# The chosen expert's weights reach the working buffers by SP transfers within SBUF instead of by VectorE copies

## The chip, the cores and the metric

One core of one Trainium2 chip runs the whole kernel. The metric is the device time of one execution in microseconds (us), the median of the runs shown. Engines are named as in the profile: PE (TensorE matmul), PEld (its weight load), DVE (VectorE), ACT (ScalarE), POOL (GpSimd), SP (SyncE, which here only issues transfers).

## The reference, cut to what matters

The input is x[16, 256, 128], 4096 tokens of 128 numbers, in fp32. A first layer (a diagonal linear recurrence over the sequence, a hidden layer of 512 with tanh-gelu, a residual, a layer norm) makes x1. A second layer is a mixture of experts:

```python
logits = xf @ Wg                       # 4096 x 8
probs = softmax(logits)
weights, indices = top_k(probs, 2)
for e in range(8):
    h = gelu(xf @ W1[e] + b1[e])       # 128 -> 512, exact gelu
    y = h @ W2[e] + b2[e]              # 512 -> 128
    out = out + y * cw[:, e:e + 1]     # cw: the two chosen weights of a token, else 0
return _layernorm(x + out)
```

## The kernel before, in words

**First layer.** Eight chunks of 512 tokens pass through `chunk(c)` on every engine. Beside them POOL splits the weights of all eight experts into a high and a low fp32r part (`weights(n)`, L410) and leaves them in one SBUF tensor, `fw[128, 8, 4*512]`: for each expert W1 high, W1 low, W2 high, W2 low. Every matmul of the kernel with these weights is three matmuls (`products`, L1015 to L1018): high by high, high by low, low by high.

**Routing.** It is done in two parts, the first 3 chunks (12 blocks of 128 tokens) and the last 5 (20 blocks). DVE finds the two chosen experts of each token and gives each (token, choice) a slot in a list sorted by expert (`route_choice`, `route_hits`, `route_ranks`, `route_slots`, `route_weights`, `route_experts`, L757 to L844). An expert's list is cut into tiles of SLOTS = 384 rows; the first part has 15 tiles, the second 21, so MT = 36, and each tile belongs to one expert. `route_experts` writes `experts`, one integer for each tile that packs the experts of tiles g, g+1 and g+2 in base 8.

**Dispatch.** POOL sends each block's rows to their slots in `slots_d` in HBM by indirect DMAs, two for each block (`dispatch`, L428 to L432): 24 in part 0, mixed with norms and weight splits, then 40 in part 1, all in a row (L460 to L463), once `routed` stands at 2 (L834) and all rows are there.

**Expert tiles.** Tile g uses the buffers of parity k = g % 2. SP loads its rows into `xb[:, k]` (`load`, L327 to L331). PE transposes them (`xt`), ACT and DVE split them into high and low (`x_high` L505, `x_low` L899), PE makes four hidden blocks (`hidden`, L1105) with `wuse[k]` planes 0 and 1, ACT applies the bias and the gelu (L569) and a high part (L574, every other one L911 on DVE), DVE the low part (L915), PE the product with W2 (L1133) with planes 2 and 3. ACT adds the output bias (L556), PE transposes back (L1119), ACT scales the rows by their routing weight into a ring `yo` of 21 tiles (L585), and POOL sends them back to `results_d` by three indirect DMAs a tile (`send_back`, L434 to L438), in order of tiles, after all 64 dispatches.

**Order.** Each engine's order is written by hand in a `step(g, ...)` of its own, walked by `walk` (L1169): steps 0 to 3 and the last ones unrolled, the others in loops of two. Routing of the second part is cut in before steps 1, 2, 3 and 4 (DVE: L957, ACT: L604). PE works one tile ahead: in step g, between the second and third W2 product of tile g, come the first two hidden blocks of tile g+1.

**The weights of a tile.** The two working buffers `wuse[0]` and `wuse[1]` (128 x 4 x 512 fp32r, 1 MB each) hold the weights of the even and the odd tile. In DVE's step g, after its work on hidden block 1, `weights2(g+1)` (L885) copies the two W2 planes of tile g+1 and the five bias columns into `buse`; after block 3, `weights1(g+2)` (L881) copies the W1 planes of tile g+2. Each `part_of_weights` (L876 to L879) is one DVE copy of 128 x 1024 fp32r; there are 72. The expert's number comes from `dve.value_load` of `experts` (L870). PE waits for `w1use_ready` before the first hidden block of a tile and for `w2use_ready` before its first W2 product. `wuse[1]` holds the first layer's weights until its last chunk is done.

**End.** SP waits until all send-backs have landed (`returned`, L355 to L361) and loads the two result rows of each token; PE, DVE, POOL and ACT add them, take the last layer norm, and SP stores. Of the results, chunks 0 to 2 need tiles 0 to 14 only and are fetched early; chunks 3 to 7 wait for the last send-back (L359).

Of the kernel before, what the change touches and what calls it, by code (L numbers as in the profile page):

```python
# [24 lines left out]
P = 128  # L25
F32 = mybir.dt.float32
# [11 lines left out]
E = 8  # L38
# [25 lines left out]
def build(nc, x, nu_log, theta_log, B_re, B_im, C_re, C_im, D_mat, W1, W2, res_logit,  # L64
# [20 lines left out]
    with ctx:  # L85
# [106 lines left out]
        expert = sb("expert", [P, MT + 2])  # L192
        pair = sb("pair", [P, MT])
        experts = sb("experts", [P, MT], I32)

        ht_h = [h_h[:, b, 0:SLOTS] for b in range(HB)]
        ht_l = [h_l[:, b, 0:SLOTS] for b in range(HB)]
# [10 lines left out]
        def y01(c):  # L208
# [18 lines left out]
            rt_ready row0_ready row1_ready lg_ready lg_sb  # L227
            hits_ready rank_ready rank_sb xin_ready xex_ready routed route_ready
            dispatched0 dispatched1 prefilled bias_loaded biasT_ready fbias_ready
            xTb_ready meta_ready w1use_ready w2use_ready xb_hi xb_lo preb_ready gelu_b hbh_ready hbh1_ready hbl_ready  # L230
            zb_ready yt_ready yT_ready yo_ready
            f_sum f_r f_st f_mv f_ve f_rstd f_nmr f_res f_res_last""".split()
        sm = {n: sem(n) for n in names}
        xr_loaded = [sem(f"xr_loaded{i}") for i in range(2)]
        fst_loaded = [sem(f"fst_loaded{i}") for i in range(2)]
        xb_loaded = [sem(f"xb_loaded{i}") for i in range(2)]

        kept = MT - YO
        GROUP = kept // 3
# [33 lines left out]
        def _(sp):  # L273
# [56 lines left out]
                wait(sp, sm["meta_ready"], g - 1)  # L330
                sp.dma_start(xb[:, k], slots_d[bass.ds(g * SLOTS, SLOTS), :].rearrange("(q p) r -> p q r", p=P)).then_inc(xb_loaded[k], 16)  # L331

            def loads(a, b):
                if (b - a) % 2:
                    load(a, a % 2)
                    a += 1
                with sp.Fori(0, (b - a) // 2) as i:
                    for k in range(2):
                        load(2 * i + (a + k), (a + k) % 2)


            sp.wait_ge(sm["dispatched0"], 16 * 2 * tiles[0])
            load(0, 0)
            load(1, 1)
            loads(2, slot0[1])
            sp.wait_ge(sm["dispatched1"], 16 * 2 * tiles[1])
            loads(slot0[1], MT)

            def results(c):

# [131 lines left out]
        def _(act):  # L482
# [76 lines left out]
            def step(g, k, now, prev, nxt, far, nth):  # L559


                if prev and not now:
                    evacuate(g - 1, 1 - k)
                if now:
                    act.wait_ge(sm["w2use_ready"], g + 1)
                    for b in range(HB):
                        act.wait_ge(sm["preb_ready"], HB * g + (b + 1))
                        wait(act, sm["hbl_ready"], HB * g + (b - 1))
                        act.activation(h32[:, b % 2, 0:SLOTS], H_PS[b % 2][:, 0:SLOTS], ACT.Gelu,  # L569
                                       bias=buse[:, k, b:b + 1]).then_inc(sm["gelu_b"], 1)  # L570
                        if b % 2 == 0:
                            act.wait_ge(sm["gelu_b"], HB * g + (b + 1))
                            wait(act, sm["zb_ready"], HB * g + (b + 1 - HB))
                            act.copy(ht_h[b], h32[:, b % 2, 0:SLOTS]).then_inc(sm["hbh_ready"], 1)  # L574
                        if b == 1 and prev:
                            evacuate(g - 1, 1 - k)
                        if b == 1 and nxt:
# [41 lines left out]
        def _(dve):  # L619
# [216 lines left out]
            def route_experts(p):  # L836

                M, g0 = slots[p], slot0[p]
                link(dve.tensor_tensor(cmp[:, 0:M, :], jio[:, 0:M].rearrange("p (m a) -> p m a", a=1).to_broadcast([P, M, E]),
                                       cnt[:, 3:4, :].to_broadcast([P, M, E]), ALU.is_ge))  # L840
                link(dve.tensor_reduce(ej[:, 0:M], cmp[:, 0:M, :], AX_X, ALU.add))
                link(dve.tensor_scalar(expert[:, g0:g0 + M], ej[:, 0:M], float(E - 1), None, ALU.min))
                link(dve.scalar_tensor_tensor(out=pair[:], in0=expert[:, 1:MT + 1], scalar=float(E), in1=expert[:, 2:MT + 2], op0=ALU.mult, op1=ALU.add))
                dve.scalar_tensor_tensor(out=experts[:], in0=expert[:, 0:MT], scalar=float(E * E), in1=pair[:], op0=ALU.mult, op1=ALU.add).then_inc(sm["route_ready"], 1)  # L844

# [27 lines left out]
                e = dve.value_load(at, min_val=0, max_val=E * E * E - 1)  # L873
                return [e // (E * E), (e // E) % E, e % E]

            def part_of_weights(k, e, a):  # L876

                return dve.tensor_copy(wuse[k][:, 2 * a:2 * a + 2, :].rearrange("p a h -> p (a h)"),  # L878
                                       fw[:, bass.ds(e, 1), 2 * a * H:2 * (a + 1) * H].rearrange("p a h -> p (a h)"))  # L879

            def weights1(g, k, e):  # L881
                wait(dve, sm["preb_ready"], HB * (g - 1))
                part_of_weights(k, e, 0).then_inc(sm["w1use_ready"], 1)

            def weights2(g, k, e):  # L885
                wait(dve, sm["zb_ready"], HB * (g - 1))
                part_of_weights(k, e, 1)
                wait(dve, sm["yt_ready"], g - 1)
                dve.tensor_copy(buse[:, k, :], fbias[:, bass.ds(e, 1), :].rearrange("p a b -> p (a b)")).then_inc(sm["w2use_ready"], 1)

            def meta(g, k):

# [12 lines left out]
            def step(g, k, now, prev, nxt, far, nth):  # L905
                if now:
                    for b in range(HB):
                        if b % 2:
                            dve.wait_ge(sm["gelu_b"], HB * g + (b + 1))
                            wait(dve, sm["zb_ready"], HB * g + (b + 1 - HB))  # L910
                            dve.tensor_copy(ht_h[b], h32[:, b % 2, 0:SLOTS]).then_inc(sm["hbh1_ready"], 1)  # L911
                            dve.wait_ge(sm["hbh1_ready"], 2 * g + (b // 2 + 1))
                        else:
                            dve.wait_ge(sm["hbh_ready"], 2 * g + (b // 2 + 1))
                        dve.tensor_tensor(ht_l[b], h32[:, b % 2, 0:SLOTS], ht_h[b].bitcast(F32), ALU.subtract).then_inc(sm["hbl_ready"], 1)  # L915
                        if b == 0 and nxt and nth != 1:

                            held[:] = experts_of(g + 1)
                        e = held[1:] if nth == 1 else held
                        if b == 1 and nxt:  # L920
                            x_low(g + 1, 1 - k)
                            weights2(g + 1, 1 - k, e[0])
                            meta(g + 1, 1 - k)
                        if b == 3 and far:
                            weights1(g + 2, k, e[1])

            for c in range(NCH):
                chunk(c)
                if c == NCH - 2:
                    dve.wait_ge(sm["fw_lo"], NFW)  # L930
                    dve.wait_ge(sm["route_ready"], 1)
                    e = experts_of(0)
                    weights1(0, 0, e[0])
                    weights2(0, 0, e[0])

            logits(NCH - 1)
            route_choice(1, 0)
            x_low(0, 0)
            weights1(1, 1, e[1])
            meta(0, 0)  # L940
            route_choice(1, 1)

# [54 lines left out]
        def _(pe):  # L997
# [100 lines left out]
            def xt(g, k):  # L1098
# [3 lines left out]
                    last = pe.transpose(XTB_PS[:, q * P:(q + 1) * P], xb[:, k, q, 0:D], ident[:])  # L1102
                last.then_inc(sm["xTb_ready"], 1)

            def hidden(g, k, b):  # L1105

                wait(pe, sm["gelu_b"], HB * g + (b - 1))
                products(H_PS[b % 2][:, 0:SLOTS], wuse[k][:, 0, b * P:(b + 1) * P], wuse[k][:, 1, b * P:(b + 1) * P],
                         xbt_h[k], xbt_l[k], True, True).then_inc(sm["preb_ready"], 1)

            def step(g, k, now, prev, nxt, far, nth):
# [7 lines left out]
                        last = pe.transpose(YB_PS[1 - k][:, q * D:(q + 1) * D], yt[:, q * P:(q + 1) * P], ident[:])  # L1119
                    last.then_inc(sm["yT_ready"], 1)  # L1120
                if now:
                    pe.wait_ge(sm["w2use_ready"], g + 1)
                    for b in range(HB):
                        if b == 2 and nxt:

                            pe.wait_ge(sm["w1use_ready"], g + 2)
                            pe.wait_ge(sm["xb_lo"], g + 2)
                            hidden(g + 1, 1 - k, 0)
                            hidden(g + 1, 1 - k, 1)
                        if b == 3 and far:  # L1130
                            xt(g + 2, k)
                        pe.wait_ge(sm["hbl_ready"], HB * g + (b + 1))
                        products(ZB_PS[k][:, 0:SLOTS], wuse[k][:, 2, b * D:(b + 1) * D], wuse[k][:, 3, b * D:(b + 1) * D],  # L1133
                                 ht_h[b], ht_l[b], b == 0, b == HB - 1).then_inc(sm["zb_ready"], 1)
# [3 lines left out]
                chunk(c)  # L1138
            logits(NCH - 1)
            xt(0, 0)  # L1140
            pe.wait_ge(sm["w1use_ready"], 1)
            pe.wait_ge(sm["xb_lo"], 1)
            hidden(0, 0, 0)
            hidden(0, 0, 1)
# [75 lines left out]
```

## Time and profile before

| what | value |
|---|---|
| runs shown | 421.11, 424.04, 427.4 us |
| median | 424.04 us |
| span of the profiled execution, first to last instruction | 403.5 us |
| median less span | 20.5 us |
| PE, DVE, ACT, POOL busy in the span | 301.3, 295.8, 259.8, 263.2 us |

The profile is of one execution and counts from its first instruction to its last. Of the profiled execution's own time only this span is shown. The 20.5 us around it hold no instruction of the profile; they are taken as the same before and after. A row of the timeline gives start (us from the span's start), duration (us), engine, line, operation, output and input, and in brackets how long the engine had been idle and what ended that. POOL's rows named DMA_INDIRECT are the time in which POOL prepares an indirect transfer, not the transfer.

### The profile page before, as it was taken

The page shows a single profiled execution, that of the slowest core. Times are in us where ns is not written, and L with a number is a line of the kernel's source. Part 1 is how long each engine was busy: PE and PEld are TensorE (multiplying, and loading weights), DVE is VectorE, ACT ScalarE, POOL GpSimd, SP SyncE. Part 2 cuts the span into 40 slices and gives each one's busy share as a digit, 9 for nine tenths or more (in the row PEclk, how much of TensorE's full clock was granted, in tenths as well). Part 3 has the DMA queues.
Part 4 walks back from the last instruction along what each step waited for, and adds up shares of the span by engine and source line. Part 5 has one row for each costly group of instructions (what it writes and reads, how often), then busy time and mean ns, then how long its engine had stood idle before and what let it go on. Part 6 is the DMA issues. An engine that isn't in the chain of part 4 may idle for free.

```text
span 403.5 us, 6693 instructions
## 1 busy us (share of the span) xinstructions
PE 301.3 (75%) x1531; PEld 253.2 (63%) x1531; DVE 295.8 (73%) x787; ACT 259.8 (64%) x569; POOL 263.2 (65%) x297
## 2 busy tenths in 40 slices
PE   2368999869874788899993599999999999100440
PEld 1235777546653677799993599999999995000110
DVE  3998999998653799899995289999999995100160
ACT  3315688378563687899994389999999993000451
POOL 4793479508877010577787777877877777777560
PEclk9999999899996699899999599999999999855585
DMA  4736516700111210223321332333333361111772
GB/s 116 268 95 220 173 39 220 281 1 33 48 47 37 56 42 20 67 74 88 87 69 54 85 92 79 85 85 83 84 89 89 92 199 52 52 52 52 190 215 78
DMA packets 47627, 39.23 MB, mean 97 GB/s; under 512 B 5160, under 2 KB 40240, under 8 KB 47608
## 3 DMA queue, kind: packets, MB, share of 16 engines
q1 hardware_dynamic: 42104, 27.68, 23.9%
q0 software_dynamic: 5504, 11.35, 8.6%
q8 instruction: 6, 0.10, 0.1%
q14 instruction: 13, 0.11, 0.1%
HBM read 18.39 MB, written 20.62 MB: 97 GB/s over the span
## 4 chain that ended last, share of the span: by engine, by line
POOL 32%; PE 29%; DVE 13%; issue 13%; ACT 6%; DMA 5%; SPq 0%; DVEq 0%; ACTq 0%; POOLq 0%
POOL slots_d L431 17%; POOL results_d L437 13%; PE bank L1016 8%; PE bank L1018 7%; PE bank L1017 7%; PE bank L1102 2%; DVE work L688 1%; PE bank L1119 1%; ACT fw L611 1%; DMA late<-slots_d 1%; DMA slots_d<-rows,slot_i 1%; ACT h L515 1%; DVE wuse L878 1%; DVE work L682 1%; DMA logs<-in_L_attn_res_logit_dram 1%
## 5 line engine op out<-in xcount | busy, mean ns | idle before, releaser
L437 POOL DMA_INDIRECT results_d<-work,dest x108 | 119.2, 1103 | 33.0 <-issue 32.0
L431 POOL DMA_INDIRECT slots_d<-rows,slot_i x64 | 72.1, 1127 | 49.4 <-DVE rows L834 19.1
L569 ACT ACTIVATE h<-bank,buse 128x384 f32<-128x384 f32 x144 | 84.1, 584 | 7.1 <-PE bank L1018 3.7
L915 DVE TENSOR_TENSOR h_l<-h,h_h 128x384 fp32r<-128x384 f32 x144 | 80.0, 556 | 6.3 <-ACT h_h L574 3.3
L1016 PE MATMUL bank<-h_h,wuse 128*128 128x384 f32 (+1 forms) x176 | 70.6, 401 | 3.9 <-DVE h_l L915 2.4
L1017 PE MATMUL bank<-h_l,wuse 128*128 128x384 f32 (+1 forms) x176 | 62.0, 352 | 0.0
L1018 PE MATMUL bank<-h_h,wuse 128*128 128x384 f32 (+1 forms) x176 | 61.9, 352 | 0.0
L1016 PE MATMUL bank<-xt_h,wuse 128*128 128x384 f32 x144 | 50.6, 351 | 3.7 <-ACT h L569 2.4
L878 DVE CAST wuse<-fw 128x1024 fp32r x72 | 49.8, 692 | 0.8 <-issue 0.8
L1017 PE MATMUL bank<-xt_l,wuse 128*128 128x384 f32 x144 | 49.5, 344 | 0.0
L1018 PE MATMUL bank<-xt_h,wuse 128*128 128x384 f32 x144 | 49.5, 344 | 0.0
L611 ACT ACTIVATE fw<-late,early 128x128 f32<-128x128 f32 x30 | 12.0, 480 | 45.0 <-POOL early L475 45.0
L1016 PEld LDWEIGHTS bank<-h_h,wuse 128*128 128x128 f32 x176 | 33.9, 192 | 9.7 <-issue 3.8
L574 ACT CAST h_h<-h 128x384 fp32r<-128x384 f32 x72 | 37.0, 514 | 4.2
L515 ACT ACTIVATE h<-bank 128x512 f32<-128x512 f32 x32 | 19.0, 594 | 29.3 <-PE bank L1018 18.0
L1017 PEld LDWEIGHTS bank<-h_l,wuse 128*128 128x128 f32 x176 | 34.0, 193 | 1.0
L1018 PEld LDWEIGHTS bank<-h_h,wuse 128*128 128x128 f32 x176 | 33.6, 191 | 1.5
L585 ACT ACTIVATE work<-bank,wslot 128x128 f32 (+1 forms) x108 | 31.5, 367 | 0.8 <-PE bank L1119 0.6
L965 DVE TENSOR_TENSOR late<-bank,work 128x512 f32<-128x512 f32 x5 | 3.4, 680 | 38.6 <-PE bank L1166 36.2
L911 DVE CAST h_h<-h 128x384 fp32r<-128x384 f32 x72 | 27.0, 375 | 6.2 <-issue 4.3
L1166 PE MATMUL bank<-work,ident 128*128 128x512 f32 x10 | 6.1, 727 | 34.0 <-DMA work<-results_d 33.9
L1016 PEld LDWEIGHTS bank<-xt_h,wuse 128*128 128x128 f32 x144 | 27.8, 193 | 5.7 <-ACT h L569 3.5
(204 smaller groups left out, 651.8 us busy)
## 6 DMA issues: line engine op xcount, KB each, us to landing
late<-slots_d SPq DMA_DIRECT2D x36, 195.0 KB
late<-in_L_ffn_W_dram SPq DMA_DIRECT2D x16, 256.0 KB, 2.8
slots_d<-zeros SPq DMA_DIRECT2D x3, 1300.0 KB, 7.8
slots_d<-zeros SPq DMA_DIRECT2D x3, 1040.0 KB, 6.8
work<-results_d SPq DMA_DIRECT2D x10, 256.0 KB, 5.5
work<-in_L_attn_x3d_dram SPq DMA_DIRECT2D x8, 256.0 KB, 3.4
out_dram<-fw SPq DMA_DIRECT2D x8, 256.0 KB, 3.1
results_d<-work,dest POOLq DMA_INDIRECT x108
```

The source lines that it names most:

```text
L431: pool.indirect_dma_start(out=slots_d, out_offset=bass.IndirectOffsetOnAxis(ap=slot_i[:, k, i:i + 1], axis=0), in_=rows[:, k, i, :], in_of ...
L437: pool.indirect_dma_start(out=results_d, out_offset=bass.IndirectOffsetOnAxis(ap=dest[:, SQ * g + q:SQ * g + q + 1], axis=0), in_=yo[:, g ...
L515: act.activation(h32[:, b % 2, :], H_PS[b % 2][:], ACT.Gelu_apprx_tanh).then_inc(sm["h_act"], 1)
L569: act.activation(h32[:, b % 2, 0:SLOTS], H_PS[b % 2][:, 0:SLOTS], ACT.Gelu, bias=buse[:, k, b:b + 1]).then_inc(sm["gelu_b"], 1)
L574: act.copy(ht_h[b], h32[:, b % 2, 0:SLOTS]).then_inc(sm["hbh_ready"], 1)
L585: last = act.activation(row_of_yo(g - 1, q), YB_PS[1 - k][:, q * D:(q + 1) * D], ACT.Copy, scale=w)
L878: return dve.tensor_copy(wuse[k][:, 2 * a:2 * a + 2, :].rearrange("p a h -> p (a h)"), fw[:, bass.ds(e, 1), 2 * a * H:2 * (a + 1) * H].rea ...
L911: dve.tensor_copy(ht_h[b], h32[:, b % 2, 0:SLOTS]).then_inc(sm["hbh1_ready"], 1)
L915: dve.tensor_tensor(ht_l[b], h32[:, b % 2, 0:SLOTS], ht_h[b].bitcast(F32), ALU.subtract).then_inc(sm["hbl_ready"], 1)
L1016: mm(out_, wh, xh, start=start, stop=False)
L1017: mm(out_, wh, xl, start=False, stop=False)
L1018: return mm(out_, wl, xh, start=False, stop=stop)
```

## The change

The 72 DVE copies go, and with them the semaphores `w1use_ready` and `w2use_ready`. SP issues 72 transfers in their place, SBUF to SBUF, 128 partitions of 4096 bytes each (512 KB), with the expert's number in a register that SP loads from a new integer tensor `expert_i`. SP's order changes with them. DVE keeps the bias copy (`biases`), and `route_experts` gets one small copy more. PE waits for the two halves by transfer semaphores of each buffer.

```diff
+        expert_i = sb("expert_i", [P, MT], I32)
...
+        w1_loaded = [sem(f"w1_loaded{i}") for i in range(2)]
+        w2_loaded = [sem(f"w2_loaded{i}") for i in range(2)]
...
-            def loads(a, b):
+            def expert_of(g):
+                at = expert_i[0:1, g:g + 1] if isinstance(g, int) else expert_i[0:1, bass.ds(g, 1)]
+                return sp.value_load(at, min_val=0, max_val=E - 1)
+
+            def part_of_weights(k, e, a):
+                return sp.dma_start(wuse[k][:, 2 * a:2 * a + 2, :].rearrange("p a h -> p (a h)").bitcast(F32),
+                                    fw[:, bass.ds(e, 1), 2 * a * H:2 * (a + 1) * H].rearrange("p a h -> p (a h)").bitcast(F32))
+
+            def weights1(g, k, e):
+                wait(sp, sm["preb_ready"], HB * (g - 1))
+                part_of_weights(k, e, 0).then_inc(w1_loaded[k], 16)
+
+            def weights2(g, k, e):
+                wait(sp, sm["zb_ready"], HB * (g - 1))
+                part_of_weights(k, e, 1).then_inc(w2_loaded[k], 16)
+
+            def tile(g, k):
+                e = expert_of(g)
+                weights1(g, k, e)
+                load(g + 1, 1 - k)
+                weights2(g, k, e)
...
+            sp.wait_ge(sm["route_ready"], 1)
+            e = expert_of(0)
+            weights1(0, 0, e)
+            weights2(0, 0, e)
             sp.wait_ge(sm["dispatched0"], 16 * 2 * tiles[0])
             load(0, 0)
             load(1, 1)
-            loads(2, slot0[1])
+            e = expert_of(1)
+            sp.wait_ge(sm["lg_ready"], NCH)
+            weights1(1, 1, e)
+            weights2(1, 1, e)
+            load(2, 0)
+            last = slot0[1] - 1
+            tiles_of(2, last)
+            e = expert_of(last)
+            weights1(last, last % 2, e)
+            weights2(last, last % 2, e)
             sp.wait_ge(sm["dispatched1"], 16 * 2 * tiles[1])
-            loads(slot0[1], MT)
+            sp.wait_ge(sm["route_ready"], 2)
+            load(last + 1, (last + 1) % 2)
+            tiles_of(last + 1, MT - 1)
...
+                link(dve.tensor_copy(expert_i[:, g0:g0 + M], expert[:, g0:g0 + M]))
...
-            def weights2(g, k, e):
-                wait(dve, sm["zb_ready"], HB * (g - 1))
-                part_of_weights(k, e, 1)
+            def biases(g, k, e):
                 wait(dve, sm["yt_ready"], g - 1)
-                dve.tensor_copy(buse[:, k, :], fbias[:, bass.ds(e, 1), :].rearrange("p a b -> p (a b)")).then_inc(sm["w2use_ready"], 1)
+                dve.tensor_copy(buse[:, k, :], fbias[:, bass.ds(e, 1), :].rearrange("p a b -> p (a b)")).then_inc(sm["buse_ready"], 1)
...
                             x_low(g + 1, 1 - k)
-                            weights2(g + 1, 1 - k, e[0])
+                            biases(g + 1, 1 - k, e[0])
                             meta(g + 1, 1 - k)
-                        if b == 3 and far:
-                            weights1(g + 2, k, e[1])
...
+            def weights_loaded(loaded, g, k):
+                pe.wait_ge(loaded[k], 8 * (g - k) + 16)
...
-                    pe.wait_ge(sm["w2use_ready"], g + 1)
+                    weights_loaded(w2_loaded, g, k)
...
-                            pe.wait_ge(sm["w1use_ready"], g + 2)
+                            weights_loaded(w1_loaded, g + 1, 1 - k)
```

## Rows read from the trace of the kernel before

**Rows 1.** Page, part 1: busy time and share of the span.

```profile
PE 301.3 (75%) x1531; PEld 253.2 (63%) x1531; DVE 295.8 (73%) x787; ACT 259.8 (64%) x569; POOL 263.2 (65%) x297
```

**Rows 2.** Windows, all engines: PE, PEld, DVE, ACT, POOL busy, clock, DMA share, GB/s.

```profile
250.00:300.00 50.00, 50.00 (x310) 48.64 (x309) 47.30 (x123) 47.92 (x114) 39.63 (x34) 1.00 0.30 83
```

**Rows 3.** Chain that ended last, in order of time: start, us, what.

```profile
373.60 2.23 DMA results_d<-work,dest
```

**Rows 4.** Groups of POOL by line: busy us, mean ns | idle before, what ended it.

```profile
L437 POOL DMA_INDIRECT results_d<-work,dest x108 | 119.2, 1103 | 33.0 <-issue 32.0 <-ACT work L585 0.9
L431 POOL DMA_INDIRECT slots_d<-rows,slot_i x64 | 72.1, 1127 | 49.4 <-DVE rows L834 19.1 <-issue 18.5 <-ACT rows L498 11.9
```

**Rows 5.** Windows of L431 alone (first), then of L437: length, busy, count.

```profile
164.20:222.60 58.40, 46.29 (x40) 0.95 0.25 73
...
222.60:336.00 113.40, 89.75 (x78) 0.96 0.34 96
336.00:374.00 38.00, 28.85 (x31) 0.69 0.17 53
```

**Rows 6.** Timeline of POOL: start, us, what.

```profile
249.19 0.96 POOL L437 DMA_INDIRECT results_d<-work,dest  x1 [0.30 <-issue]
252.07 1.09 POOL L437 DMA_INDIRECT results_d<-work,dest  x1 [0.30 <-issue]
254.93 1.63 POOL L437 DMA_INDIRECT results_d<-work,dest  x1 [0.31 <-issue]
322.86 1.03 POOL L437 DMA_INDIRECT results_d<-work,dest  x1 [0.30 <-issue]
```

**Rows 7.** Timeline of DVE at the same times.

```profile
249.63 0.36 DVE L911 CAST h_h<-h 128x384 fp32r<-128x384 f32 x1 [0.39 <-issue]
252.24 0.35 DVE L911 CAST h_h<-h 128x384 fp32r<-128x384 f32 x1
255.76 0.68 DVE L878 CAST wuse<-fw 128x1024 fp32r x1
```

**Rows 8.** Windows of L878 alone: length, busy, count.

```profile
164.20:222.60 58.40, 13.93 (x20) 0.95 0.25 73
222.60:336.00 113.40, 28.36 (x41) 0.96 0.34 96
```

**Rows 9.** Timeline of ACT: the last work on two tiles in a row.

```profile
261.36 0.87 ACT L585 ACTIVATE work<-bank,wslot 128x128 f32 x3
266.23 0.88 ACT L585 ACTIVATE work<-bank,wslot 128x128 f32 x3
```

**Rows 10.** Chain that ended last: the first DVE copy on it, of five before 164 us.

```profile
141.66 0.69 DVE wuse L878
```

**Rows 11.** Timeline of ACT and DVE ahead of the second dispatch.

```profile
155.51 0.69 DVE L878 CAST wuse<-fw 128x1024 fp32r x1
156.11 0.44 DVE L814 TENSOR_TENSOR late<-late,cnt 128x160 f32<-128x160 f32 x1
158.96 0.58 ACT L569 ACTIVATE h<-bank,buse 128x384 f32<-128x384 f32 x1 [1.54 <-DVE h_l L915]
162.65 0.35 ACT L532 ACTIVATE early<-early 128x180 f32<-128x180 f32 x1
163.04 0.32 DVE L831 TENSOR_REDUCE den<-early 128x20 f32<-128x160 f32 x1
```

**Rows 12.** Timeline of ACT: the last work on the last tile.

```profile
337.31 0.88 ACT L585 ACTIVATE work<-bank,wslot 128x128 f32<-128x128 f32 x3 [0.64 <-PE bank L1119]
```

**Rows 13.** Windows, all engines, at the highest DMA share; columns as in rows 2.

```profile
65.00:70.00 5.00, 5.00 (x20) 3.41 (x19) 4.77 (x8) 4.76 (x12) 4.76 (x6) 1.00 1.05 358
321.00:325.00 4.00, 4.00 (x26) 3.92 (x26) 3.93 (x12) 3.87 (x9) 3.12 (x3) 1.00 0.82 235
```

**Rows 14.** DMA issues: KB each, median us to landing.

```profile
slots_d<-zeros SPq DMA_DIRECT2D x3, 1300.0 KB, 7.8
late<-in_L_ffn_W_dram SPq DMA_DIRECT2D x16, 256.0 KB, 2.8
```

More of the change, by code:

```diff
@@ L229, in build @@
             dispatched0 dispatched1 prefilled bias_loaded biasT_ready fbias_ready
-            xTb_ready meta_ready w1use_ready w2use_ready xb_hi xb_lo preb_ready gelu_b hbh_ready hbh1_ready hbl_ready
+            xTb_ready meta_ready buse_ready xb_hi xb_lo preb_ready gelu_b hbh_ready hbh1_ready hbl_ready
             zb_ready yt_ready yT_ready yo_ready
@@ L331, in load, with tiles_of @@
                 sp.dma_start(xb[:, k], slots_d[bass.ds(g * SLOTS, SLOTS), :].rearrange("(q p) r -> p q r", p=P)).then_inc(xb_loaded[k], 16)
-            def loads(a, b):
+            def expert_of(g):
[15 more added lines that the diff above has]
+                weights2(g, k, e)
+            def tiles_of(a, b):
                 if (b - a) % 2:
-                    load(a, a % 2)
+                    tile(a, a % 2)
                     a += 1
@@ L338, in loads @@
                     for k in range(2):
-                        load(2 * i + (a + k), (a + k) % 2)
+                        tile(2 * i + (a + k), (a + k) % 2)
+            sp.wait_ge(sm["route_ready"], 1)
+            e = expert_of(0)
+            weights1(0, 0, e)
+            weights2(0, 0, e)
             sp.wait_ge(sm["dispatched0"], 16 * 2 * tiles[0])
@@ L344, in _ @@
             load(1, 1)
-            loads(2, slot0[1])
-            sp.wait_ge(sm["dispatched1"], 16 * 2 * tiles[1])
-            loads(slot0[1], MT)
+            e = expert_of(1)
[8 more added lines that the diff above has]
+            weights2(last, last % 2, e)
+            sp.wait_ge(sm["dispatched1"], 16 * 2 * tiles[1])
+            sp.wait_ge(sm["route_ready"], 2)
+            load(last + 1, (last + 1) % 2)
+            tiles_of(last + 1, MT - 1)
+            e = expert_of(MT - 1)
+            weights1(MT - 1, (MT - 1) % 2, e)
+            weights2(MT - 1, (MT - 1) % 2, e)
             def results(c):
@@ L564, in step @@
                 if now:
-                    act.wait_ge(sm["w2use_ready"], g + 1)
+                    act.wait_ge(sm["buse_ready"], g + 1)
                     for b in range(HB):
@@ L874, in experts_of @@
                 return [e // (E * E), (e // E) % E, e % E]
[L876 to L883, printed above, removed]
-            def weights2(g, k, e):
-                wait(dve, sm["zb_ready"], HB * (g - 1))
-                part_of_weights(k, e, 1)
+            def biases(g, k, e):
                 wait(dve, sm["yt_ready"], g - 1)
-                dve.tensor_copy(buse[:, k, :], fbias[:, bass.ds(e, 1), :].rearrange("p a b -> p (a b)")).then_inc(sm["w2use_ready"], 1)
+                dve.tensor_copy(buse[:, k, :], fbias[:, bass.ds(e, 1), :].rearrange("p a b -> p (a b)")).then_inc(sm["buse_ready"], 1)
             def meta(g, k):
@@ L932, in _ @@
                     e = experts_of(0)
-                    weights1(0, 0, e[0])
-                    weights2(0, 0, e[0])
+                    biases(0, 0, e[0])
             logits(NCH - 1)
@@ L938, in _ @@
             x_low(0, 0)
-            weights1(1, 1, e[1])
             meta(0, 0)
@@ L1140, in _ @@
             xt(0, 0)
-            pe.wait_ge(sm["w1use_ready"], 1)
+            weights_loaded(w1_loaded, 0, 0)
             pe.wait_ge(sm["xb_lo"], 1)
```

## The prediction

> **What bounds the kernel now.** Busy shares first [rows 1]: PE is the busiest and DVE comes next, POOL has 65%. In the steady part of the expert tiles PE is busy 50.00 of 50 us at full clock, DVE 47.30 [rows 2]. Read like that, PE sets the pace there and a relieved DVE would bring nothing. But the chain that ended last says otherwise. It reaches the end of the expert part over POOL's send-backs, one after the other, up to the landing of the last one at 373.60 [rows 3]. The last work on the last tile is done by ACT at 337.31 + 0.88 = 338.2 [rows 12]. A tile needs three send-backs, so a POOL that kept up would be done some 4 us after that; it is done 35 us after. It is some ten tiles behind.
>
> How long has it been behind? The groups of POOL [rows 4]: before its 108 send-backs it was idle 33.0 us in all, 32.0 of it the fixed 0.3 us between two instructions; only 0.9 us was put down to waiting for ACT. Before the 64 dispatches it idled 19.1 us for DVE L834, the one wait for the second routing, which ends at 164.27. From there to 373.3 POOL never stands: 40 dispatches and 108 send-backs in a row. The chain lists PE, ACT and DVE in the middle of that stretch, but with POOL's idle time this small they hold nothing up. So the end is POOL's start at 164.27, plus 148 instructions, plus what follows the last landing (30 us), which the change leaves alone.
>
> What does one of the 148 cost? At best 0.96 us, as at 249.19 [rows 6], with the gap 1.26. Summed by windows [rows 5]: the 40 dispatches take 46.29 us, where 40 x 0.96 = 38.4, so 7.9 us more. The send-backs up to 336 take 89.75 us; one of the 78 lies there with only 0.26 us, so the quiet price is 77 x 0.96 + 0.26 = 74.2, and 15.6 us are on top. After 336, when the expert tiles are over, 31 of them, one again cut by the window's edge, take 28.85 us, which is 30 x 0.96: nothing on top. POOL thus loses **23.5 us** to something that happens while the tiles run.
>
> The timelines of POOL and DVE, held side by side, say to what. The send-back at 254.93 took 1.63 us; the weight copy L878 ran from 255.76 to 256.44, and the send-back ended at 256.56, 0.12 after the copy [rows 6, 7]. The send-back at 249.19 had the small cast L911 from 249.63 to 249.99 inside it and took 0.96, nothing extra; that at 252.07 had one from 252.24 to 252.59 and took 1.09, 0.13 more [rows 6, 7]. Big copies stop POOL, small casts do so little or not at all.
>
> The Trainium skill has a rule for this (SBUF — State Buffer, section "SBUF: two separate sides"): while DVE runs a copy in a two-port mode, GpSimd is locked out of the shared SBUF port pair and cannot write the descriptors of its own DMAs. By that rule the row at 254.93 is what must happen.
>
> **The change part by part.**
>
> *The 72 copies leave DVE.* In POOL's stretch there are 20 + 41 = 61 of them, 13.93 + 28.36 = 42.3 us of DVE time [rows 8]. What is left of DVE's work that can stop POOL is two casts L911 a tile, also about 61, and some copies of 0.16 us. I price each L911 at 0.1 us, between the 0 and the 0.13 of [rows 6, 7], nearer the upper since without the long copies they will fall on other moments of POOL's instructions: 61 x 0.1 = 6.1 us. POOL's loss goes from 23.5 to 6.1: **17.4 us gained**. Ends: nothing, if something else takes the copies' place, and all 23.5.
>
> *POOL's start at 164.27.* Before it the routing of the second part runs on DVE between the first tiles, and five copies lie on the chain, the first at 141.66 [rows 10]. Taking one out saves 0.60 us, since the instruction behind a copy starts 0.60 after it (155.51 to 156.11) [rows 11]. The last two of the five bring nothing: ACT's exp, which DVE's L831 at 163.04 needs, ends at 162.65 + 0.35 = 163.00, and ACT's own run there goes back to 158.96, where it was waiting for DVE [rows 11]. What counts is the three copies ahead of 158.96: 3 x 0.6 = **1.8 us**. Ends: -2 us, if the first tiles' weights come late, and 5 x 0.6 = 3.0.
>
> *SP's transfers.* Two of 512 KB a tile. What they cost depends on three things.
>
> First, DMA time. The tile period is 266.23 - 261.36 = 4.87 us [rows 9]; the DMA engines are busy 0.30 of it [rows 2], 1.46 us. No transfer within SBUF is in the trace. Low end: in the stretch where the engines were fully busy they moved 358 GB/s [rows 13], so 1.05 MB is 2.9 us and the sum 4.4. High end: between 256 KB in 2.8 us and 1300 KB in 7.8 [rows 14] there are 1044 KB in 5.0 us, so 1024 KB is 4.9 us and the sum 6.4, more than a tile period. I take the low end, because the added pieces are 4 KB long, like or longer than those of that stretch. It fits into 4.87, with little room.
>
> Second, delay. W2 of tile g is issued when PE has finished tile g-2 and needed one period plus two hidden blocks later, about 6 us; 2.8 + 256 KB at the high end's slope, 1.2, is 4.0 us [rows 14]. W1 has about 1.5 periods, 7.3 us. Both are hidden behind PE's work; if that cover goes, PE waits 1 us for each us of lateness, every tile. Rows for tile g+1 (`load`) now stand behind W1 of tile g on SP, and behind its wait for tile g-2's hidden blocks, which are done before the other waits of `load`; PE needs those rows in the second half of the next step. Behind the wait of W2 stands the next tile's `value_load` and W1, which have time. After the second dispatch `load(15)` goes first.
>
> Third, who pays. POOL is behind, so PE may slow down without cost. With the gain POOL would be done at 373.3 - 19.2 = 354.1. The copy at 141.66 [rows 10] belongs to the end of tile 0's step, so I count from 142: 35 more periods, and a tail of 6.3 us (an estimate: some 2.5 from the last product to the end of ACT's L585, and three send-backs of 1.26) reach 354 at a period of (354.1 - 148.3) / 35 = 5.9 us. So I cost the transfers at nothing up to 5.9 us a tile.
>
> *The added DVE copy* of the experts' numbers is 0.2 us, twice: the first under ACT and POOL's work of the first dispatch, the second behind L834, off the path. *PE's waits* are as many as before. The final part is as it was.
>
> **Sum:** 17.4 + 1.8 = 19.2 us; the span goes from 403.5 to 384.3, and with the same 20.5 us around it the time from 424.04 to **404.8 us**. The median is taken as belonging to this span; the three runs lie within 3 us or so of it.
>
> **The rivals.**
>
> *A. The casts take over.* If L911 stopped POOL for all the time that they overlap, each would cost 0.36 x 0.96 / 1.26 = 0.27 us, 61 of them 16.5; the gain is 23.5 - 16.5 + 1.8 = 8.8 and the time 415.2. For it: the 1.09 at 252.07. Against it: the 0.96 at 249.19 with a whole cast inside. The Trainium skill stands on this side (same page, section "Who interferes with whom"): a cast in such a mode makes the other side block fully. The row at 249.19 does not agree.
>
> *B. POOL is slowed by the transfers themselves.* Then it loses as much as before, and only the 1.8 us remain: 422.2. Against it: between 321 and 325 the DMA engines were 82% busy [rows 13], and the send-back at 322.86 took 1.03 [rows 6].
>
> *C. The transfers cost their high end.* PE's period becomes 6.4: 142 + 35 x 6.4 + 6.3 = 372.3 against 373.3, the time 423. The end is PE's then.
>
> *D. Slower: the DMA engines become the bound.* If a byte that leaves SBUF and enters it again costs twice the low end, the tile needs 1.46 + 5.9 = 7.3 us, 142 + 35 x 7.3 + 6.3 = 403.8, 30 us more: 454. It decides from a period of (373.3 - 148.3) / 35 = 6.4 on. For it: the engines are already 30% busy, 36 x 1 MB is nearly what the whole kernel moves now, and `wuse` has just two buffers. Against it: nothing but the 358 GB/s of another kind of transfer.
>
> **How the numbers follow.** Forecast 0.62 (own range 399 to 412: the gain from 12 to 25). A 0.12, B 0.07, C 0.08, D 0.11. A measurement of this kernel can tell about 2%, 8.5 us, from no change, so faster is below 415.6: the forecast and a little over half of A, 0.69. B, C and the rest of A are within 2%: 0.20. D: 0.11. The range 399 to 422 takes the forecast, A and most of B, and leaves out D, most of C and an improvement beyond 25 us.
>
> **What would show it.** DMA_INDIRECT means near 1.0 us during the tiles, where they are 1.15 now; POOL's second dispatch starting near 162.5; the last send-back near 354; POOL still with nothing but 0.3 us gaps; the tile period still 4.9 us and PE's row without waits for transfers; DMA share near 0.9 in the tiles. The prediction is wrong if POOL's instructions stay at 1.15 us (B), or PE waits for `wuse` transfers in every tile and ends later than 350 (C, D).

## The result, and the profile after

The changed kernel took **433.11 us** (430.74 to 437.66, 5 runs) beside 425.02 us for the kernel before (421.11 to 427.4, 5 runs): ratio 1.019, 95% interval 1.014 to 1.025. It is 1.9% slower, against 4.5% faster in the forecast (404.8 us). The ratios and intervals of this document leave out executions over 1.5% above the fastest of their kernel, so a ratio can differ from that of the two medians. The page of the changed kernel, its span, its engines, then PE and POOL over 40 slices of 10.8 us, busy tenths, and POOL's send-backs:

```profile
span 431.2 us, 6792 instructions
PE 310.2 (72%) x1531; PEld 253.0 (59%) x1531; DVE 259.4 (60%) x717; ACT 261.4 (61%) x569; POOL 249.1 (58%) x297
...
PE   2389998789746896430011599999999999999850
...
POOL 4696298258781106777775155665555556557751
...
L483 POOL DMA_INDIRECT results_d<-work,dest x108 | 109.7, 1016 | 79.8 <-ACT work L631 55.2
```

PE's 301.3 of [rows 1] have hardly moved, DVE's 295.8 are 259.4 now. In the slices there is a hole in PE's row, 4 3 0 0 1 1, that POOL's 7s run beside. But the span is 431.2 where that of before was 403.5, and only 1.9 us lie around it, not 20.5. So the profile that the prediction read and the times beside it were two different things, and the first question is what. Three stretches, all engines, columns as in [rows 2]:

```profile
164.20:222.60 58.40, 16.61 (x63) 13.22 (x63) 8.76 (x26) 10.71 (x24) 44.38 (x47) 0.61 0.28 93
222.60:250.00 27.40, 8.90 (x42) 8.35 (x43) 5.49 (x17) 7.48 (x17) 11.37 (x12) 0.58 0.25 88
250.00:395.00 145.00, 141.11 (x834) 129.41 (x833) 99.17 (x276) 130.78 (x307) 85.81 (x83) 1.00 0.79 275
```

In the first stretch POOL works on: 47 instructions in 58.4 us, as good as without any gap but the 0.3 us. PE makes 63 matmuls. DVE and ACT stand too, and the DMA engines are 28% busy. It begins with the second dispatch, and from 250 on PE is busy 141.11 of 145 us at full clock. ACT's waits from 160 to 260 (line, what it waited for, us, times, longest):

```profile
ACT h L615 <- remote: 34.4, 4, 22.9
ACT rt L602 <- remote: 16.5, 2, 12.8
ACT work L631 <- remote: 8.2, 1, 8.2
```

"Remote" stands where nothing that this core's engines did just then accounts for the release. 59 us of this are a **stall** in which POOL alone moves. When it is over, the tiles set the pace and POOL waits for ACT, 55.2 us in all before its send-backs where it was 0.9 in [rows 4]. One of them takes 1.016 us, as forecast for a relieved POOL (1.103 in [rows 4]), but POOL's own pace no longer ends the kernel.

### The profile page after: what moved, and what is told of

It reads as the page before. It is cut to its first block, busy times and chain, and to the rows that moved or that the text cites. A ratio compares the mean times of both kernels' runs of the same rounds, so it can differ in the third digit from the quotient of the medians.

```text
span 431.2 us, 6792 instructions
## 1 busy us (share of the span) xinstructions
PE 310.2 (72%) x1531; PEld 253.0 (59%) x1531; DVE 259.4 (60%) x717; ACT 261.4 (61%) x569; POOL 249.1 (58%) x297
## 4 chain that ended last, share of the span: by engine, by line
PE 30%; DVE 17%; another core or an unknown queue 14%; issue 11%; ACT 10%; POOL 9%; DMA 5%; SPq 1%; ACTq 1%; DVEq 0%; POOLq 0%
PE bank L1048 9%; PE bank L1050 9%; PE bank L1049 8%; POOL slots_d L477 5%; ACT h L615 3%; DVE h_l L738 2%; DVE work L734 2%; PE bank L1134 2%; POOL results_d L483 2%; PE bank L1155 2%; DMA work<-results_d 1%; DMA late<-slots_d 1%; ACT h L561 1%; DVE h_l L951 1%
## 5 line engine op out<-in xcount | busy, mean ns | idle before, releaser
L483 POOL DMA_INDIRECT results_d<-work,dest x108 | 109.7, 1016 | 79.8 <-ACT work L631 55.2
L477 POOL DMA_INDIRECT slots_d<-rows,slot_i x64 | 66.1, 1033 | 48.3 <-issue 18.5
L1048 PE MATMUL bank<-xt_h,wuse 128*128 128x384 f32 x144 | 53.8, 374 | 50.9 <-issue 43.9
L1050 PE MATMUL bank<-xt_h,wuse 128*128 128x384 f32 x144 | 49.9, 346 | 0.0
L602 ACT ACTIVATE rt<-bank,buse 128x384 f32<-128x384 f32 x36 | 20.8, 577 | 19.4 <-remote 16.5
L937 DVE TENSOR_TENSOR xt_l<-bank,xt_h 128x384 fp32r<-128x384 f32 x36 | 19.9, 552 | 18.1 <-ACT xt_h L554 14.5
L1155 PE MATMUL bank<-ident,rt 128*128 128x128 f32 x108 | 18.6, 282 | 16.3 <-ACT rt L602 15.8
L738 DVE TENSOR_TENSOR h_l<-h,h_h 128x512 fp32r<-128x512 f32 x32 | 26.1, 839 | 4.1 <-ACT h_h L564 3.1
```

The costliest lines, as they stand in the source:

```text
L477: pool.indirect_dma_start(out=slots_d, out_offset=bass.IndirectOffsetOnAxis(ap=slot_i[:, k, i:i + 1], axis=0), in_=rows[:, k, i, :], in_of ...
L483: pool.indirect_dma_start(out=results_d, out_offset=bass.IndirectOffsetOnAxis(ap=dest[:, SQ * g + q:SQ * g + q + 1], axis=0), in_=yo[:, g ...
L738: dve.tensor_tensor(h_l[:, b, :], h32[:, b % 2, :], h_h[:, b, :].bitcast(F32), ALU.subtract).then_inc(sm["hl_ready"], 1)
L1048: mm(out_, wh, xh, start=start, stop=False)
L1050: return mm(out_, wl, xh, start=False, stop=stop)
```

## The experiments

**Relief alone, bytes alone, transfers beside the copies.** First, is the stall made by POOL's gain, by the bytes, or by the transfers' presence? The first kernel is the one before with DVE's copies cut to 4 columns from tile 2 on:

```diff
-                return dve.tensor_copy(wuse[k][...], fw[...])
+                n = 2 * H if isinstance(g, int) and g < 2 else 4
+                return dve.tensor_copy(wuse[k][...][:, 0:n], fw[..., 2 * a * H:2 * a * H + n]...)
```

> The kernel before, but from tile 2 on each of DVE's two weight copies moves only 4 of its 1024 columns, so the tiles compute with the wrong expert's weights: the copying is left out, all waits stay, no transfer is added. Theory 'transfers': the stall of PE behind 168.8 us in the changed kernel comes from SP's transfers, and the gain of 17 to 25 us that POOL gets is real; then there is no stall here, the second dispatch's and the send-backs' instructions take about 1.0 us, the last send-back is near 354 us on the scale of the old profile, and the time is 15 to 25 us below the kernel before (ratio 0.94 to 0.965). Theory 'POOL': PE's signals are held up because POOL now issues its indirect transfers without pauses; then the stall of some 60 us in tiles 5 and 6 is here too, and the time is at or above that of before (ratio 1.0 to 1.03).

The second is the changed kernel with `n = 128` columns in each of SP's transfers, in the same way.

> The changed kernel, but from tile 2 on each of SP's weight transfers moves 128 of its 1024 columns (an eighth of the bytes), so the tiles compute with wrong weights for the rest: most of the copying is left out, all waits and issues stay. Theory 'bytes of the transfers': no stall, time 15 to 25 us below the kernel before. Theory 'POOL without pauses' and theory 'SP's new waits or issues': the stall between about 169 and 240 us is still there and the time stays near 433 (ratio 1.0 to 1.03).

The third has both DVE's copies and SP's transfers:

```diff
+        spare = [tables[:, 736 * n:736 * (n + 1)] for n in range(2)]
...
-                return sp.dma_start(wuse[k][...], fw[...])
+                return sp.dma_start(spare[a], fw[..., 2 * a * H:2 * a * H + 736]...)
...
+            def part_copied(k, e, a):
+                return dve.tensor_copy(wuse[k][...], fw[...])
```

> The changed kernel with DVE's weight copies put back as in the kernel before, and SP's transfers kept but sent to a spare buffer, 736 of the 1024 columns each (72% of the bytes), none for tile 0; PE waits for both. So POOL is slowed by DVE's copies as before, and the transfers come on top. Theory 'transfers': the stall of PE in tiles 5 and 6 is here, and the time is 20 to 60 us above before. Theory 'POOL without pauses': no stall, since DVE's copies give POOL its pauses; the time is within 2% of before, POOL again the bound with 1.1 to 1.15 us an instruction.

Measured beside 404.61 us (13 runs) for the kernel before: 390.3 (ratio 0.965, 0.960 to 0.970), 388.18 (0.962, 0.958 to 0.967) and 407.59 (1.006, 1.000 to 1.011). No stall in any, and the two relieved kernels gain as forecast in kind, 14 and 16 us. (What makes the 2 us between them wasn't tested.) Read alone this says that the stall needs full transfers and a relieved POOL together. But the kernel before took 404.6 us here and 425.0 in the first comparison: this was another chip, and nothing can be concluded before both kernels have run on the same one.

**The changed kernel again, and half the bytes.** The half is `n = 512`.

> The changed kernel once more, unaltered, beside the kernel before on a chip where that takes 404.6 us (the 425 us of the first comparison came from elsewhere). If the stall of PE behind the second dispatch belongs to the change, it is here too, 50 to 70 us long, and the time is 8 to 30 us above that of before. If it belonged to the one chip or to that moment, it is gone, and the time is where the two runs without the copying on DVE lie: 388 to 395 us, ratio 0.96 to 0.98.

> The changed kernel, but from tile 2 on each of SP's transfers moves 512 of the 1024 columns (half the bytes, pieces of 2 KB), so the tiles compute with wrong weights for the rest: half of the copying is left out. If the bytes that the DMA engines move decide, the stall is here but shorter than with all bytes, or gone below some load: time between 388 and that of the changed kernel. If the number or the order of SP's transfers and waits decided, the run with an eighth of the bytes would have shown it already, so 388 us is expected by every theory in which the bytes play no part, and then the changed kernel beside it must also be fast.

Before: 425.29 us. Changed: 436.65 (ratio 1.027, 1.016 to 1.038), half the bytes: 435.56 (1.019, 1.007 to 1.032), both with the stall. So this is a chip on which before takes 425 us, as in the first comparison, and half of the bytes makes no difference that the intervals can tell.

**Before, changed and relief alone on one chip.**

> The kernel before, unaltered, with a profile, on the chip that this call gets: so far the kernel before took 425 us on one chip and 404.6 on another, and the profile that the prediction read had a span of 403.5. Where it takes 425 us here, theory 'the chip's stall' expects the stall of PE behind the second dispatch in this profile too (about 20 us of lost time at the end, 50 us or more of idle PE that POOL's lateness partly covers); theory 'the change makes the stall' expects no idle time of PE there and another reason for the 20 us. Where it takes 404.6 us, the profile is as the one that was read.

> The changed kernel on the same chip. Where before takes 404.6 us, theory 'the chip's stall' expects no stall of PE here and 388 to 393 us, ratio 0.96 to 0.97; theory 'the change makes the stall' expects the stall and 415 us or more. Where before takes 425 us, both expect 433 to 437.

> The kernel before with DVE's weight copies cut to 4 columns from tile 2 on (the copying is left out), no transfers, again. Where before takes 404.6 us it should repeat 390 us. Where before takes 425 us, theory 'the chip's stall' expects PE's stall here too, of the length that it has with SP's transfers, and 425 to 435 us; theory 'the transfers make it worse' expects a time below 412 us.

Before took 431.68 us (13 runs), changed 441.11 (1.022, 1.017 to 1.028), relief alone 428.82 (0.998, 0.992 to 1.004). And the profile of the kernel *before*, on this chip, page and windows:

```profile
span 431.1 us, 6693 instructions
...
PE   2288999789676988433001199999999999999850
...
POOL 5695098248870106777777136666666666667851
```

```profile
164.20:222.60 58.40, 19.76 (x90) 16.29 (x90) 15.38 (x41) 14.79 (x34) 44.87 (x45) 0.67 0.20 61
222.60:250.00 27.40, 4.95 (x14) 3.94 (x15) 3.57 (x10) 4.64 (x11) 12.64 (x14) 0.50 0.11 34
250.00:395.00 145.00, 142.66 (x832) 130.72 (x832) 129.05 (x329) 130.38 (x303) 93.38 (x83) 0.99 0.31 84
```

The stall is there without the change. It goes with the chip: in the experiments of this section the kernel before took 404 to 405 us on three chips, call them **A**, and 425 to 432 on three others, **B**. One B chip came up in two comparisons and was B in both (431.68 and 428.61 us); the others ran in one comparison each. The profile read for the prediction has A's span (403.5; A's runs take some 2 us more than their span), the 424.04 us and the rest of the first comparison are B's. The traces tell the kinds apart too: for the kernel before, this one holds 3766 records of semaphore increments, and the one read for the prediction 6325. All traces taken on B in this document have 3733 to 4308, all others taken on A 6343 or more. The timeline of the kernel before on B shows what the stall is made of:

```profile
180.29 0.33 PE L1018 MATMUL bank<-xt_h,wuse 128*128 128x384 f32 x1
180.67 0.56 DVE L915 TENSOR_TENSOR h_l<-h,h_h 128x384 fp32r<-128x384 f32 x1
...
189.16 0.34 PE L1018 MATMUL bank<-xt_h,wuse 128*128 128x384 f32 x1
189.23 0.56 DVE L915 TENSOR_TENSOR h_l<-h,h_h 128x384 fp32r<-128x384 f32 x1 [2.98 <-issue]
190.23 0.96 POOL L431 DMA_INDIRECT slots_d<-rows,slot_i  x1 [0.30 <-issue]
...
194.02 0.96 POOL L431 DMA_INDIRECT slots_d<-rows,slot_i  x1 [0.30 <-issue]
195.13 0.58 ACT L569 ACTIVATE h<-bank,buse 128x384 f32<-128x384 f32 x1 [5.93 <-remote]
...
228.13 0.58 ACT L569 ACTIVATE h<-bank,buse 128x384 f32<-128x384 f32 x1 [23.57 <-remote]
```

L569 needs PE's hidden block (`preb_ready`) and DVE's low part of an earlier block (`hbl_ready`). Counted off by blocks, the L569 at 195.13 needs the PE block that ended at 180.62 and the DVE row that ended at 181.2; the increment of the PE block is recorded at 195.10, over 14 us later. The PE and DVE rows at 189 are what the next L569 needs, and that one starts at 228.13. From 189.8 to 195.13 only POOL has rows. The rest of the trace's semaphore records say the same. These are PE's, ACT's and DVE's increments that have a record within 0.06 us of their instruction's end:

| stretch, us | POOL's indirect transfers | B | A, profile of before |
|---|---|---|---|
| 0 to 90 | none | 281 of 281 | 283 of 283 |
| 92 to 128 | first dispatch | 80 of 123 | 116 of 116 |
| 130 to 160 | none | 142 of 142 | 147 of 147 |
| 170 to 240 | end to end | 22 of 71 | 331 of 331 |
| 250 to 390 | on B three a tile, then a pause | 465 of 771 | 576 of 577 |

Many of the missing ones have no record of their own (37 records for the 71 increments from 170 to 240), so the counts say that they are not there in time, and only some say by how much they are late. On B an increment can come late where POOL prepares indirect transfers.

What the change costs on B is read behind the stall. ACT's scaling of rows for the eighth tile and for the last, in the kernel before, changed, and relieved, on this one chip:

```profile
256.46 0.88 ACT L585 ACTIVATE work<-bank,wslot 128x128 f32 x3
...
399.31 0.88 ACT L585 ACTIVATE work<-bank,wslot 128x128 f32<-128x128 f32 x3 [0.64 <-PE bank L1119]
```

```profile
255.32 0.87 ACT L631 ACTIVATE work<-bank,wslot 128x128 f32 x3
...
405.50 0.88 ACT L631 ACTIVATE work<-bank,wslot 128x128 f32<-128x128 f32 x3 [0.64 <-issue]
```

```profile
254.51 0.88 ACT L585 ACTIVATE work<-bank,wslot 128x128 f32 x3
...
394.88 0.88 ACT L585 ACTIVATE work<-bank,wslot 128x128 f32<-128x128 f32 x3 [0.64 <-PE bank L1119]
```

From the start of the last to the end of the span it is 31.8 to 32.3 us in each. The change comes 6.2 us later than before, and 10.6 later than relief alone. In these three profiles taking DVE's copies away is worth 4.4, and SP's transfers cost 10.6. (The medians on this chip, 431.68, 441.11 and 428.82, put the copies at 2.9 and the transfers at 12.3; the interval of relief alone, 0.992 to 1.004, includes no gain at all.) The stall ends at nearly the same time in all three, as the eighth tile shows. The loss lies in the 28 tiles behind it: 142.9 us before, 150.2 changed, 140.4 relieved. Single executions scatter: the two other B profiles of the full change took 143.8 and 145.5 us for the same tiles.

**Pacing POOL.** If POOL's unbroken stream starves the others, holding it to the tiles' pace should dissolve the stall:

```diff
+            def paced(n):
+                pool.wait_ge(sm["gelu_b"], 16 + 17 * n // 20)
...
+                    if p == 1:
+                        paced(2 * (i - tile0[1]) + k)
...
+                    paced(2 * tiles[1] + SQ * g + q)
```

> The kernel before, with POOL's stream from the second dispatch on held to the pace of the tiles: its n-th instruction waits until ACT has made 16 + 0.85 n activations L569 (of 144). Nothing is left out. Theory 'POOL's unbroken stream holds up the other engines' signals on some chips': where before takes 425 us or more, the stall of 70 us is gone or is a few us, PE works through it, and the time falls to 395 to 415 us (ratio 0.92 to 0.97). Rival 'something else in that moment (instruction fetch, clock, the table load) stops PE': the stall stays, POOL waits too, ratio 0.99 to 1.04. Where before takes 404.6 us there is no stall to remove and both expect 0.99 to 1.02.

> The changed kernel with the same pacing of POOL. Where before takes 425 us or more, theory 'unbroken stream' expects the stall gone and 390 to 415 us, POOL relieved of DVE's copies and therefore the same as or up to 10 us below the paced kernel before; the rival expects 430 to 445 us. Where before takes 404.6 us: as the changed kernel without pacing.

> The changed kernel unaltered, for the chip that this call gets. Where before takes 425 us or more: 433 to 441 again. Where before takes 404.6 us (not seen yet for this kernel): POOL is the bound there and gets 14 to 16 us back, as the two runs with the copying left out did, and the transfers at full size may take back some of it: 388 to 396 us.

> The changed kernel with transfers of 128 of the 1024 columns from tile 2 on (seven eighths of the copying left out), again. Where before takes 425 us or more: if the bytes cost the 5 to 9 us by which the change is slower there, this is 425 to 430 us, like the run with DVE's copies cut; if the number of transfers, issues and signals costs it, it is 433 to 441 us like the changed kernel. Where before takes 404.6 us: 388 us as before.

This was an A chip (before 404.04 us). Paced before 404.73 (1.000, 0.997 to 1.003), paced after 390.08 (0.964, 0.959 to 0.969), and for the first time the changed kernel on A: **391.86 us, ratio 0.970, 0.962 to 0.979**. An eighth of the bytes: 386.65 (0.958, 0.952 to 0.963). The pair of paced kernels ran again:

> The kernel before with POOL's stream from the second dispatch on held to the pace of the tiles: its n-th instruction waits until ACT has made 16 + 0.85 n activations L569. Nothing is left out. Where before takes 425 us or more: theory 'POOL's unbroken stream' expects the stall of 70 us gone or a few us and 395 to 415 us (ratio 0.92 to 0.97); rival 'something else of that moment' expects it to stay, ratio 0.99 to 1.04. Where before takes 404 us: 0.99 to 1.01 as measured once.

> The changed kernel with the same pacing. Where before takes 425 us or more: theory 'unbroken stream' expects 390 to 415 us, the rival 430 to 445 us. Where before takes 404 us: 390 us as measured once.

It was an A chip once more (before 405.31): 406.23 (1.003, 0.999 to 1.006) and 390.53 (0.967, 0.961 to 0.973). And a third time:

> The kernel before with POOL held to the pace of the tiles. Where before takes 425 us or more: theory 'POOL's unbroken stream' expects the stall of 70 us gone or a few us and 395 to 415 us; rival 'something else of that moment' expects 425 us or more with the stall in the profile. Where before takes 404 us: 404 to 406 us, as measured twice.

> The changed kernel with the same pacing. Where before takes 425 us or more: theory 'unbroken stream' expects 390 to 415 us, the rival 430 to 445 us. Where before takes 404 us: 390 us, as measured twice.

Now a B chip, before 428.61 us: paced before 435.19 (ratio 1.014, 1.000 to 1.028), paced after 437.62 (1.020, 1.009 to 1.031). The stretches of the paced kernel before, and ACT's waits from 164 to 395:

```profile
164.20:222.60 58.40, 42.77 (x213) 38.51 (x213) 35.19 (x93) 35.55 (x80) 39.05 (x36) 0.85 0.23 65
222.60:250.00 27.40, 21.66 (x113) 18.67 (x112) 18.06 (x47) 18.36 (x44) 18.54 (x17) 0.94 0.22 60
250.00:395.00 145.00, 114.86 (x594) 102.90 (x593) 94.47 (x235) 94.72 (x217) 95.24 (x88) 0.88 0.27 77
```

```profile
ACT h L575 <- remote: 25.3, 14, 3.6
ACT rt L562 <- remote: 19.8, 8, 4.1
ACT h L575 <- PE bank L1024: 17.8, 15, 2.2
```

The theory's mechanism holds and its number fails. The long stall is gone: 213 matmuls in the first stretch instead of 90, no remote wait over 4.1 us where there was one of 23.6. So it was POOL's stream that made PE stand, and the rival of "that moment" falls. But the time is not won: behind 250 PE makes 594 matmuls where it made 832, and ACT's remote waits there come to 28.4 us where they were 3.3. Why is open. POOL makes about as many instructions there (88 for 83), and a like share of the increments is in time (315 of 542 from 250 to 390, for 465 of 771). What differs is how they lie: three after each tile and then a pause in the kernel before, more spread when paced.

**Bytes or number on B.**

> The changed kernel with transfers of 128 of the 1024 columns from tile 2 on (seven eighths of the copying left out). Where before takes 425 us or more: 'bytes' expects a ratio of 0.99 to 1.0, like the kernel with DVE's copies cut (0.9975); 'number of transfers and signals' expects 1.015 to 1.025, like the changed kernel. Where before takes 404 us: a ratio of 0.96, as measured twice.

> The changed kernel with transfers of 512 of the 1024 columns from tile 2 on (the lower halves of the split weights stay those of an earlier tile). Where before takes 425 us or more: 1.015 to 1.025, as measured once (1.0193). Where before takes 404 us: if the 5 us between full size and an eighth go with the bytes, half is near 389 us; if they come only when the DMA engines are nearly full, it is 387.

Before 425.23 us on a third B chip: an eighth of the bytes 437.3 (430.73 to 443.49 in 4 runs; 1.017, 1.007 to 1.028), half 437.15 (1.026, 1.018 to 1.034), for 1.019 to 1.027 at full size. So the bytes are not what costs the 2%. Relief alone stood at 0.998, on another B chip. By exclusion what costs some 2% on B comes with the rest of the change: SP's 72 issues, their waits and completion signals, or the new order of SP's loads. No run separates these, and why A and B differ stays open as well.

## Why the prediction was wrong, by its own steps

**"The same 20.5 us around it", "the median is taken as belonging to this span": this step failed.** Every run that was measured later lies 1.7 to 3.3 us above its span. The 20.5 us were some 2 us and the difference between two kinds of chip. It also hid that the bound that I derived was A's. On B, POOL stands 55.2 us waiting for ACT's rows, so the whole chain "POOL's start plus 148 instructions" is not what ends there: relief alone, which was to bring 17.4 us, brought 2.9 there, within the noise, and what the transfers add came on top.

On A the prediction can be judged step by step. The changed kernel there; groups of POOL, the window as in [rows 2], and the landing as in [rows 3]:

```profile
L483 POOL DMA_INDIRECT results_d<-work,dest x108 | 112.2, 1039 | 32.9 <-issue 32.0 <-ACT work L631 0.9
L477 POOL DMA_INDIRECT slots_d<-rows,slot_i x64 | 67.1, 1048 | 48.7 <-issue 18.5 <-DVE rows L880 18.4 <-ACT rows L544 11.8
```

```profile
250.00:300.00 50.00, 50.00 (x309) 48.58 (x308) 37.22 (x103) 47.83 (x115) 38.73 (x38) 1.00 0.89 305
```

```profile
360.80 2.22 DMA results_d<-work,dest
```

- *POOL bounds the kernel, with nothing but 0.3 us gaps*: right on A, idle 32.9 us, 32.0 of it issue, as in [rows 4].
- *POOL's start 1.8 us earlier*: right, 162.38 for 164.27.
- *The period stays, no PE waits for weights, DMA share near 0.9*: right. PE is busy 50.00 of 50, the share 0.89. The low end of the DMA price held, 0.89 x 4.87 = 4.3 us a tile for the 4.4 forecast. Rivals C and D fall: the sign of D came on B, its mechanism didn't, since there the share is 0.79 and an eighth of the bytes is as slow.
- *17.4 us off POOL's 148 instructions*: too large. The last landing came from 373.60 to 360.80, 12.8 earlier, 1.9 of it the start; the gain is 10.9, and of the 23.5 us on top 12.6 are left where 6.1 were forecast.
- *The casts L911 cost 6.1 us*: not refuted, and rival A's 16.5 us fall. With an eighth of the bytes the last landing is earlier still:

```profile
356.04 2.23 DMA results_d<-work,dest
```

  That is 17.6 us, 1.7 of it the start, so 7.6 are left for the casts, DVE's other small copies and an eighth of the bytes together. POOL and DVE in the changed kernel on A, two send-backs with a cast inside:

```profile
249.81 1.29 POOL L483 DMA_INDIRECT results_d<-work,dest  x1 [0.30 <-issue]
...
252.67 0.96 POOL L483 DMA_INDIRECT results_d<-work,dest  x1 [0.30 <-issue]
```

```profile
250.19 0.36 DVE L947 CAST h_h<-h 128x384 fp32r<-128x384 f32 x1
...
253.00 0.36 DVE L947 CAST h_h<-h 128x384 fp32r<-128x384 f32 x1 [0.39 <-issue]
```

  The first took 0.33 on top, the second nothing. In these two rows, then, a cast costs up to 0.33, perhaps by where it falls; the ends taken from two rows before were 0 and 0.13. The Trainium skill, "SBUF — State Buffer", section "Who interferes with whom", says that of a cast in a two-port mode and a GpSimd instruction whichever issues first has the shared ports for its whole instruction, and the other blocks fully. These rows do not agree: POOL's instruction began first in both, and yet it was the one that grew longer in the first, while the cast took 0.36 us both times. The send-back at 254.93 in [rows 6, 7] had begun before its copy too.
- *The transfers cost nothing*: this is the term that was mis-sized, and B was the rival that named it. 12.6 - 7.6 = 5.0 us come with the other seven eighths of the bytes, 0.03 us an instruction; the times say the same, 391.86 - 386.65 = 5.2. The prediction had dismissed the transfers' cost by one send-back of 1.03 us [rows 6]: 0.07 too much, times 148, would have been 10. Relief alone, with no transfer at all, was hardly faster than the changed kernel on A: 390.3 us, ratio 0.965 for 0.970, the intervals overlapping. In its profile, of an execution of 395.29 us, a send-back took 1.045 us, for 1.039 in the changed kernel and 1.008 with an eighth of the bytes, so the copies of 4 columns that DVE keeps there seem to cost POOL something too; that was not tested.
- *30 us behind the last landing, unchanged*: right, 390.2 - 360.8 = 29.4.

On A the sum is then 1.9 + 10.9 = 12.8 us in the profile and 12.2 in the medians, for 19.2 forecast: the mechanism was right there and the gain too large. On B, where the comparison was run, it is a loss of 8.1 us.

## What to carry to other kernels

Before you subtract from a measured time, set the profile's span beside it: if they differ by more than the few microseconds that other runs show, the profile is of another situation, and the bound in it may not be the bound of the run that counts. Ask how far each engine is from being the bound when another is held up; here a stall that made the kernel some 20 us longer turned a POOL-bound kernel into a tile-bound one. Moving work from an engine to transfers frees the engine, but adds bytes, issues and signals. On A the bytes cost 5 of the 17 us gained; on B something other than the bytes cost some 2%.

## What the runs showed that was not expected

Three chips of six ran the same kernel 5 to 7% slower, always in the same place. On these, semaphore increments of PE, ACT and DVE arrive late while POOL prepares indirect transfers (22 of 71 in time from 170 to 240, against 331 of 331), and they are in time again when it prepares none (142 of 142). Where POOL's instructions stand end to end, ACT waits up to 23.6 us in one piece. The granted clock stands at 0.50 (1.2 of 2.4 GHz) from 222.6 to 250 in the kernel before on B, behind a stretch in which PE was busy 19.8 of 58.4 us, and at 0.99 after 250. The stall ends some 8 us after POOL's last instruction of the row (232.59 + 0.95, then ACT's work again from 241.7 on and PE's from 242.4 on in the changed kernel); why not at once stays open. On A, two transfers within SBUF of 512 KB a tile, in pieces of 4 KB, brought the DMA engines to a share of 0.89 (0.30 before) without slowing PE, which was busy 50.00 of 50 us.
